# Layer 1 copies its turned rows one step later, the edge GRU has sixteen slots, the dense half is dealt out 52, 50, 47, 47

## What is computed

```python
h = maximum(layernorm(x), 0)
x = x + L0(h)   # three SAGE layers: h @ W_self.T + b + (segment_sum(h[src], dst) / deg) @ W_neigh.T, relu between
h = maximum(layernorm(x), 0)
x = x + L1(h)   # mean over in-edges and out-edges of h - edge_attr, three products, batch norm
h = maximum(layernorm(x), 0)
x = x + L2(h)   # messages h[src] @ W_msg.T + embed[type], summed by dst, then a GRU cell on every node
h = maximum(layernorm(x), 0)
x = x + L3(h)   # mean over out-edges of (h @ W.T + b)[dst]
```

## Time and profile before

| what | us |
|---|---|
| three runs | 5606.28, 5615.59, 5625.59; median 5615.59 |
| profiled execution, its own time | 5624.52 |
| its span in the trace | 5622.7 |
| layer 1 | 990 to 1318 |
| edge GRU | 4663 to 5201 |
| four stages with dense groups | 153 to 425, 425 to 687, 1318 to 1604, 1787 to 2073 |
| busy share of the span | PE 79%, DVE 65%, POOL 63%, ACT 50% |

### The profile page before, as it was taken

One profiled execution on the slowest core, in us unless ns is written; L12 is line 12 of the kernel. 1 busy time (PEld: TensorE's weight loads), 2 busy tenths in 40 slices (PEclk: granted clock), 3 DMA queues, 4 the chain that ended last, 5 costly groups with the idle time before them and its releaser, 6 DMA issues. The chain is left out here.

```text
span 5622.7 us, 105014 instructions
## 1 busy us (share of the span) xinstructions
PE 4422.8 (79%) x24681; PEld 3303.8 (59%) x24851; DVE 3646.9 (65%) x13944; ACT 2810.0 (50%) x6163; POOL 3554.6 (63%) x3627
## 2 busy tenths in 40 slices
PE   5889877668989988436767557999999798775874
PEld 3666555446866877336655435666666685443774
DVE  7878866556856868544377557999999104443652
ACT  0788766556844865432211103888888223222431
POOL 1677676654712740575777813888888675777687
PEclk9999999889999999658999889999999658887887
DMA  3555577656878869555777599888888334443664
GB/s 108 187 186 194 189 236 225 211 189 225 290 247 286 291 235 338 180 156 187 244 187 152 97 235 249 287 285 284 284 285 273 105 115 145 146 147 101 140 119 62
DMA packets 712469, 1139.12 MB, mean 203 GB/s; under 512 B 103156, under 2 KB 373347, under 8 KB 711970
## 3 DMA queue, kind: packets, MB, share of 16 engines
q1 hardware_dynamic: 536154, 908.74, 49.8%
q0 software_dynamic: 134400, 161.92, 14.0%
q10 hardware_dynamic: 41736, 66.50, 3.2%
HBM read 625.98 MB, written 532.56 MB: 206 GB/s over the span
## 5 line engine op out<-in xcount | busy, mean ns | idle before, releaser
L1186 POOL DMA_INDIRECT G_V<-layer_rows,i_tb x400 | 379.1, 948 | 414.2 <-POOLq L277 266.5
L1210 PE MATMUL bank<-first_last_indicators,G_V 125*128 (+1 forms) x1600 | 267.5, 289 | 180.1 <-DVE G_V L1956 180.0
L2736 POOL TENSOR_TENSOR P_gA<-P_x,bn_scale 128x512 f32<-128x512 f32 x196 | 250.4, 1278 | 226.8 <-DMA P_x<-node_table 202.9
L2129 POOL DMA_INDIRECT out<-O_out,i_srcf x200 | 319.0, 1595 | 105.4 <-issue 56.4
L1186 POOL DMA_INDIRECT G_x<-node_table,i_src x200 | 191.9, 960 | 304.6 <-POOLq L277 244.0
L2129 POOL DMA_INDIRECT node_table<-H_out,H_rows_of_src x200 | 323.0, 1615 | 90.6 <-issue 56.5
L1210 PEld LDWEIGHTS bank<-first_last_indicators,G_V 125*128 125x128 f32 x1600 | 271.3, 256 | 184.2 <-issue 128.6
L1661 PE MATMUL bank<-B_S,B_V 127*128 127x125 f32 x2000 | 294.8, 295 | 44.6 <-DVE B_S L1637 33.6
L2817 ACT ACTIVATE P_xh<-P_xh,P_nb,P_rs 128x128 f32<-128x128 f32 x784 | 320.3, 479 | 0.0
L1661 PEld LDWEIGHTS bank<-B_S,B_V 127*128 127x128 f32 x2000 | 270.2, 209 | 55.3 <-issue 48.9
L1096 POOL DMA_INDIRECT degree_and_position<-es_posf,es_i_position x200 | 194.7, 974 | 161.2 <-DMA dst_keys<-dst_keys 100.5
(11 more groups left out here) (479 smaller groups left out, 13965.3 us busy)
## 6 DMA issues: line engine op xcount, KB each, us to landing
P_x<-node_table SPq DMA_DIRECT2D x196, 512.0 KB
x_and_h<-P_xh SPq DMA_DIRECT2D x195, 512.0 KB, 6.0
B_V<-values SPq DMA_DIRECT2D x250, 256.0 KB, 3.1
BN_g<-node_table SPq DMA_DIRECT2D x195, 256.0 KB
out<-P_out SPq DMA_DIRECT2D x195, 256.0 KB
node_table<-G_xg SPq DMA_DIRECT2D x97, 512.0 KB, 3.2
values<-G_V SPq DMA_DIRECT2D x150, 256.0 KB, 3.1
layer_rows<-A_a SPq DMA_DIRECT2D x100, 256.0 KB, 3.3
```

What stands on the lines that cost most here:

```text
L1186: pool.indirect_dma_start(out=rows[u][:, c, :], out_offset=None, in_=table, in_offset=index_of(index, i, c)).then_inc(landed[u], 16)
L1210: last = nc.tensor.matmul(m.bank[7][:, bass.ds((i * TILE + c) * 2, 2)], V[0:EP, c, :], m.ind[0:EP, bass.ds(i * TILE + c, 1), :].rearrange( ...
L2129: pool.indirect_dma_start(out=table, out_offset=index_of(index, i, c), in_=out[u][:, c, :], in_offset=None, bounds_check=table.shape[0] - ...
L2736: nc.gpsimd.tensor_tensor(t[v % 2][:], x[v][:, :, D:2 * D], m.Arow[:].unsqueeze(1).to_broadcast([128, TILE, D]), ALU.mult)\
```

## The change

Three edits that don't depend on each other.

1. In layer 1 DVE copies the turned result of group i - 5 in step i, and no longer that of i - 4; SP's store of these rows moves along. Both loops get one step more at the end (n + 4 for n + 3), and DVE's loop keeps one more step straight at its start (back 9 for 8).
2. In the GRU there are sixteen slots of gathered rows for eight. POOL gathers group i + 10 for i + 2 in step i, still after `fin` of i - 6. The loops of SP, DVE, ACT and PE have sixteen steps a turn for eight, since a slot's number has to be a constant in the body.
3. The dense groups are dealt out 52, 50, 47, 47 to the four stages for 49 each.

```diff
@@ -35,7 +35,7 @@
 EG = TILE * EP
 LN_EPS = 1e-5
 TYPES = 9
-CHUNKS = 4
+SHARES = (52, 50, 47, 47)
 KEY_BITS = 11
 KEY = 1 << KEY_BITS
 
@@ -558,8 +558,8 @@
 
 
     groups = -(-m.N // ROWS)
-    first = chunk * groups // CHUNKS
-    dense = DenseFirst(nc, m, a, P, first, (chunk + 1) * groups // CHUNKS - first)
+    first, end = (sum(SHARES[:k]) * groups // sum(SHARES) for k in (chunk, chunk + 1))
+    dense = DenseFirst(nc, m, a, P, first, end - first)
 
     def sweeps(eng, own, other, first_other=False):
         together(eng, ([other(eng)] if other and first_other else []) + ([own(eng)] if own else []) + ([other(eng)] if other and not first_other else []),
@@ -1515,11 +1515,12 @@
                         sp.dma_start(edge_rows(m.XD, i), xd_whole[w][:]).then_inc(s_xo[w], 16)
                     if has(i + 1):
                         value_load(sp, m, f, i + 1, (u + 1) % 4, V, s_V, s_agg)
-                    if has(i - 4):
-                        f.after(s_r, i - 4)
-                        sp.dma_start(edge_rows(table, i - 4), rows_whole[u][:]).then_inc(s_ro[u], 16)
-
-                sweep(sp, -1, n, n + 3, body, unroll=8, back=5, ahead=1, special=0)
+                    if has(i - 5):
+                        v = (u - 5) % 4
+                        f.after(s_r, i - 5)
+                        sp.dma_start(edge_rows(table, i - 5), rows_whole[v][:]).then_inc(s_ro[v], 16)
+
+                sweep(sp, -1, n, n + 4, body, unroll=8, back=5, ahead=1, special=0)
                 finish(sp, s_xo, n)
                 finish(sp, s_oo, n)
                 finish(sp, s_ro, n)
@@ -1534,13 +1535,14 @@
                     if has(i - 1):
                         ln.finish(f, i - 1, (u - 1) % 4)
                         row_selectors(nc, m, f, i - 1, (u - 1) % 4, bK, S, s_row, s_sel, s_agg)
-                    if has(i - 4):
-                        f.after(s_T, i - 4)
-                        f.landed(s_ro, i - 8, u)
-                        nc.vector.tensor_copy(rows[u][:], bR[u % 2][0:EP, :].rearrange("p (c f) -> p c f", c=TILE)).then_inc(s_r, 1)
+                    if has(i - 5):
+                        v = (u - 5) % 4
+                        f.after(s_T, i - 5)
+                        f.landed(s_ro, i - 9, v)
+                        nc.vector.tensor_copy(rows[v][:], bR[v % 2][0:EP, :].rearrange("p (c f) -> p c f", c=TILE)).then_inc(s_r, 1)
 
                 clear_pads(nc, P, dve)
-                sweep(dve, 0, n, n + 3, body, unroll=8, back=8, ahead=0, special=0)
+                sweep(dve, 0, n, n + 4, body, unroll=8, back=9, ahead=0, special=0)
 
             @block.scalar
             def _(act):
@@ -2554,17 +2556,17 @@
                         f.after(s["fin"], i - 5)
                         sp.dma_start(edge_rows(m.XD, i - 5), out_whole[v][:]).then_inc(s_o[v], 16)
 
-                sweep(sp, -4, n, n + 4, body, unroll=8, back=5, ahead=4, special=0)
+                sweep(sp, -4, n, n + 4, body, unroll=16, back=5, ahead=4, special=0)
                 finish(sp, s_o, n)
 
             @block.gpsimd
             def _(pool):
                 f = Flow(pool, lambda g: 0 <= g < n)
-                for i in range(-2, n + 6):
-                    if f.has(i + 2) and i + 2 >= targets.fetched:
-                        w = (i + 2) % 8
+                for i in range(-10, n + 6):
+                    if f.has(i + 10) and i + 10 >= targets.fetched:
+                        w = (i + 10) % 16
                         f.after(s["fin"], i - 6)
-                        gather(pool, f, m.i_dst, i + 2, w, m.X2H, targets.whole, targets.landed)
+                        gather(pool, f, m.i_dst, i + 10, w, m.X2H, targets.whole, targets.landed)
                     if f.has(i - 6):
                         f.after(s["fin"], i - 6)
                         scatter(pool, f, m.i_dstf, i - 6, (i - 6) % 4, m.out, out_whole, s_sc)
@@ -2579,7 +2581,7 @@
                         f.after(s["back"], i - 5)
                         f.landed(s_o, i - 9, v)
                         f.landed(s_sc, i - 9, v, 64)
-                        nc.vector.tensor_tensor(out[v][:], bB[0:np_, :].rearrange("p (c f) -> p c f", c=TILE), x[(u - 5) % 8][:, :, 0:D], ALU.add)\
+                        nc.vector.tensor_tensor(out[v][:], bB[0:np_, :].rearrange("p (c f) -> p c f", c=TILE), x[(u - 5) % 16][:, :, 0:D], ALU.add)\
                           .then_inc(s["fin"], 1)
                     if has(i - 3):
                         v = (u - 3) % 4
@@ -2606,7 +2608,7 @@
                         nc.vector.tensor_tensor(hnm[v % 2][:], rn[v % 2][:], bI[:, 0:W], ALU.add).then_inc(s["rn"], 1)
 
                 clear_pads(nc, P, dve)
-                sweep(dve, -2, n, n + 4, body, unroll=8, back=9, ahead=2, special=0)
+                sweep(dve, -2, n, n + 4, body, unroll=16, back=9, ahead=2, special=0)
 
             @block.scalar
             def _(act):
@@ -2636,14 +2638,14 @@
                         f.after(s["q"], i - 5)
                         nc.scalar.activation(z[v][:], bZ[:, 0:W], ACT.Sigmoid, bias=m.col["b_z"]).then_inc(s["z"], 1)
 
-                sweep(act, 0, n, n + 4, body, unroll=8, back=9, ahead=0, special=0)
+                sweep(act, 0, n, n + 4, body, unroll=16, back=9, ahead=0, special=0)
 
             @block.tensor
             def _(pe):
                 def body(i, u, has):
                     f = Flow(pe, has)
                     if has(i):
-                        w = u % 8
+                        w = u % 16
                         f.landed(targets.landed, i, w, 64)
                         f.after(s["hT"], i - 1)
                         for c in range(TILE):
@@ -2671,7 +2673,7 @@
                         f.after(s_ac, i - 1)
                         add_up(nc, m, f, i + 1, (u + 1) % 4, V, S, bA[(u + 1) % 2], s_V, s_sel, s_agg)
 
-                sweep(pe, -1, n, n + 3, body, unroll=8, back=5, ahead=1, special=0)
+                sweep(pe, -1, n, n + 3, body, unroll=16, back=5, ahead=1, special=0)
 
 
 def gru_dense(nc, m, a):
@@ -3022,7 +3024,7 @@
         self_and_incoming(nc, m, a)
         batch_norm(nc, m, a)
         gru_dense(nc, m, a)
-        targets = RowsAhead(nc, m, "x2_and_h_of_targets", m.i_dst, m.X2H, 2 * D, 8)
+        targets = RowsAhead(nc, m, "x2_and_h_of_targets", m.i_dst, m.X2H, 2 * D, 16)
         messages(nc, m, a, targets)
         gru(nc, m, a, targets)
         targets.stack.close()
```

## The result

The changed kernel takes 5520.86 us (median of 5510.77 to 5524.41) against 5619.86 us of the kernel before in the same comparison: a ratio of 0.9824, 95% interval 0.9801 to 0.9848. The forecast was 5495 with a range of 5472 to 5550. Measured once more beside the experiments, the same code gave 5513.27 against 5623.11, 0.9811 (0.9795 to 0.9828).

The account below looks back on a forecast made before the run. Layer 1 was taken as bound by PE-DVE waits, the GRU by POOL. Layer 1 -83, GRU -20 and dense half -17.8 sum to -121 us, from a median of 5615.6 to 5495, range 5472 to 5550 (8 in 10).

Parts of the forecast that it names:

- What bounds it: Whole kernel: no engine busy throughout; layer 1 bound by waits between PE and DVE, the edge GRU by POOL.
- Layer 1, -83: Layer 1: moving the copy cuts the PE-DVE loop, POOL's gathers then set the end; -83 us, range 50 to 87.
- GRU, -20: Edge GRU: sixteen slots remove POOL's 21.90 us wait ahead of group 8's gather; taken as -20 us.
- the working's own 18 to 28: GRU's end: between POOL's 5163 and the gates' 5173, against 5190.93 today, a gain of 18 to 28 us.
- POOL's bound alone: GRU tail: sixteen scatters at 5.15 us a group after 5081 end at 5163, the 28 us end of the range.
- Dense half, -17.8: Dense groups 52, 50, 47, 47: positions 0, lookup +4, both takes -10.9 each; -17.8 us, range -20 to -8.
- The floor under them: Takes: the next stage can't start until 10.9 us after POOL's last transfer, about 1592, just covering -10.9 each.
- The sum, -121: Whole kernel: -83 - 20 - 17.8 = -121 us, a median of 5495; own range -133 to -80.
- PE at half clock setting layer 1's pace: Layer 1: PE takes 5.47 us a step throughout, -35 instead of -83, total -73, 5543 us; chance 0.12.
- Layer 1 unchanged: Layer 1: another wait replaces the loop, only GRU and dense half gain, -38, 5578 us; chance 0.08.
- The GRU's gates eating the gain: GRU: the gates fall behind in the tail and give back the 20 us, 5515 us; chance 0.06.
- Longer loops that cost: GRU: sixteen-step bodies reach PE, DVE and ACT too slowly; at 15 us a step total +32, 5648; chance 0.03.

Follow-up runs that it names:

- the kernel with the added wait: Changed kernel with the GRU's difference, product and new h reading the gates' sums in PSUM, so DVE waits for them: GRU 553.2 us for 517.5.

## Why the forecast held, point by point

**What bounds it.** Layer 1 by a loop of waits, the GRU by POOL, read from the earlier trace rows: both held. The copy alone gives 82 us in its stage, with nothing else changed.

**Layer 1, -83: measured -83.9.** From the stage's first instruction it is -83.1. The steps of the working stand as they were put. The loop is cut (10.0 us of waits for 142.4), the next limit is POOL's 4.99 us a group, the last statistics begin 2.4 us behind the last gather (2 were taken), the tail is 18.2 us (18.9 were taken). DVE alone is faster than I put it, 3.65 us and not 3.9, and PE, put at 3.82 us, keeps up with 3.64 when sixteen groups are gathered ahead. The exact agreement is partly luck: the old layer 1 of the profile on which the forecast rests was the longest of three.

**GRU, -20: measured -15.8.** The mechanism was right: a wait of 21.9 us, gone, to be had with twelve slots as well. The size is below the working's own 18 to 28, and two terms were off, against each other. The end was put near the gates' pace in the tail, 8 us above POOL's own; but POOL waits for nobody there, so the gates did not set the end, and POOL's bound alone would have been -28. And POOL's gather and scatter were taken at their means of before, 10.5 us a step, as if these were prices of the instructions. They hold a part that depends on where DVE stands: 10.3 us without, and 10.7 in the changed kernel, where DVE, now waiting for scatters, stands at the same place in each step, and one of eight transfers always begins inside the new h. From first gather to last scatter POOL took 509.9 us, 11 more than the working's bound for it: 6 in the 34 steps of gather and scatter, about 3 in the tail, 2 ahead of the first scatter. Seen from before, POOL's busy time rose from 388.4 to 393.2 us for the same 384 instructions, so 21.9 us of wait came back as 16.9 at the last scatter. That the forecast of -20 came near is partly luck. The first scatter came 20 us later and not 13, as the gather of group 16 stands ahead of it, which the working left out; that moves no end.

**Dense half, -17.8: measured -15.4.** Positions hidden, lookup +5 for +4, takes -8.3 and -11.7 for -10.9 each. The mechanism held: two steps of 5.36 us are gone, and the last dense store comes 9.7 and 11.8 us earlier in the two takes. The floor under them did not bind with 47 groups (13.1 us behind POOL's last gather, where 10.9 were the floor); it was 2 us too high, as shown above.

**The sum, -121: measured -99 and -110.** The changed stages give -115 and -114 in the two profiles of the changed kernel. The rest of the first result's distance is in stages that the change does not touch: add_incoming was 10 us long in the profiled execution and within 1 us of before in the second. Why it is now and then 10 us longer was not looked into. The forecast was made against one execution, and untouched stages were given no spread of their own; the range had room for it.

**The rivals.** PE at half clock setting layer 1's pace (0.12): its condition did not occur, the granted clock rose to 0.97. Its price was also too low: the 5.47 us were read from a step that ran at half clock only in part, as the two products of L1601 take 1.00 us in both steps of the earlier trace rows (one alone takes 0.58 us in most steps of the stage, 0.91 in the slowest). The Trainium skill, "TensorE: Matmul & The Clock Gate", Part 1, whose rule I weighed there, has activity release the throttle; the trace agrees, since PE was busy for 193.6 of 245 us and the granted clock rose. Layer 1 unchanged (0.08): no. The GRU's gates eating the gain (0.06): no, though the kernel with the added wait shows the mechanism, at 9 to 11 us a group in place of some 7. Longer loops that cost (0.03): no, 532.2 for 533.3.

## What to carry to other kernels

When two engines feed each other in one step, ask which of their operations can be taken from the step before; one copy moved by a step was worth 75 to 84 us here, and the next limit could be read beforehand from what the other engines need alone. More slots help a queue that is already the bound only where it stands still: find that one wait, and buy just enough depth to fill it (twelve slots did what sixteen do). And look for the queue's idle time elsewhere in the program: ten groups gathered while POOL had nothing to do took another 41 us out of layer 1 (27 off the median).

## What the hardware showed that I had not expected

**An issue on POOL is held back by DVE.** A gather or scatter that begins while DVE reads two tiles in SBUF takes longer by what is left of DVE's operation, less some 0.1 us: up to 1.4 us for 0.95 in the changed kernel's gathers. Before the change three scatters that began 0.1 us ahead of such an operation took 1.65 to 1.70 us for 0.98. With one of the inputs in PSUM none is lengthened: 10.3 us a step for 10.7. The Trainium skill, "SBUF — State Buffer", section "Who interferes with whom", says that a DVE instruction with two SBUF inputs contends with a GpSimd instruction that reads SBUF; the trace agrees, and gives the size for the issue of an indirect transfer. The same section has a probe in which a `tensor_tensor` did not stall transfers; the 136 issues counted here did wait for one, and the measurement decides for this case.

**The granted clock rose in both changed stages, in one of them with no more work for PE.** Layer 1 went from 0.89 to 0.97 with PE busy for 79% of the stretch and not 68%; the GRU from 0.86 to 0.91 with PE at 73% in place of 74%. There PE's work comes in even steps now, of 10.7 us, in place of pairs, some 7 and then 11 to 16 us apart. That the evenness does it is not shown.

**The same code of a plain stage differs by up to 13 us from profile to profile** (add_incoming 443.6 to 456.5), more than some of the effects that were looked for: the stage table settled what the medians alone could not.
